# Statistics by VectorE for one batch, another order of first loads, centering in halves, and new written-out orders in a fused attention and FFN kernel

## The reference

```python
def layernorm(x):                       # over the last axis
    return (x - mean(x)) / sqrt(var(x) + 1e-5)

def mx_dequant(t):                      # blocks of 32 along the last axis
    scale = maximum(max_abs_of_block / 448, 1e-30)
    return (t / scale).astype(float8_e4m3fn).astype(float32) * scale

def attention(logits, ctx):
    q, k = ctx @ Wq.T + bq, ctx @ Wk.T + bk
    return logits @ softmax(q @ k.T).T  # x_m[l, m] = sum_n logits[l, n] * p[m, n]

def ffn(x, gate_w, up_w, down_w):
    linear = lambda a, w: mx_dequant(a) @ mx_dequant(w).T
    return linear(silu(linear(x, gate_w)) * linear(x, up_w), down_w)

x = x + attention(layernorm(x), ctx)
x = x + ffn(layernorm(x), gate_w, up_w, down_w)
```

## Time and profile before

| | us |
|---|---|
| median of 3 runs | 611.59 |
| lowest and highest | 611.04, 611.65 |
| profiled execution, its own time | 611.49 |
| span of its instructions | 609.7 |
| TensorE matmuls busy | 602.0 |
| VectorE busy | 485.4 |
| ScalarE busy | 308.9 |
| GpSimd busy | 48.8 |

### The profile page before, as it was taken

How to read it: one execution, slowest core, us unless ns; L and a number is a source line. 1 busy time by engine, 2 the same in 40 slices (tenths; PEclk the granted TensorE clock), 3 DMA queues, 4 the chain that set the end, 5 groups by cost and what they waited for, 6 DMA issues and landing times.

```text
span 609.7 us, 7213 instructions
## 1 busy us (share of the span) xinstructions
PE 602.0 (99%) x2690; PEld 282.8 (46%) x2690; DVE 485.4 (80%) x455; ACT 308.9 (51%) x463; POOL 48.8 (8%) x60
## 2 busy tenths in 40 slices
PE   8999999999999999999999999999999999999998
PEld 3455545444444444444444444444444444444446
DVE  5998998899999979899899997231148989799940
ACT  3989989553455545863572642421212512644521
POOL 0000100201100100102001100000000000110000
PEclk9999999999999999999999999999999999999999
DMA  8967989989888868775566668600110452856681
GB/s 326 384 144 263 293 229 213 258 216 250 207 206 207 209 135 176 172 158 130 130 118 140 162 140 147 137 4 15 18 19 0 90 86 51 137 90 102 119 141 34
DMA packets 148162, 92.28 MB, mean 151 GB/s; under 512 B 134304, under 2 KB 134688, under 8 KB 143264
## 3 DMA queue, kind: packets, MB, share of 16 engines
q1 hardware_dynamic: 142656, 63.78, 44.5%
q0 software_dynamic: 5472, 28.05, 19.8%
HBM read 25.76 MB, written 8.39 MB: 56 GB/s over the span
## 4 chain that ended last, share of the span: by engine, by line
PE 89%; ACT 7%; DMA 2%; issue 1%; SPq 0%; DVE 0%; DVEq 0%; ACTq 0%
PE bank L713 54%; PE bank L725 17%; PE bank L728 8%; PE bank L697 5%; PE bank L744 2%; ACT h L952 1%; DMA W<-hT 1%; PE bank L688 1%; ACT h L943 1%; PE bank L673 1%; DMA gu_lo<-in_consts 1%; PE bank L681 1%; ACT hT L932 1%; ACT mag L908 1%; ACT hT L994 0%
## 5 line engine op out<-in xcount | busy, mean ns | idle before, releaser
L713 PE MATMUL bank<-gu_hi,xT 128*128 128x512 f16 x1024 | 243.5, 379 | 1.0 <-DVE gu_hi L1440 1.0
L713 PEld LDWEIGHTS bank<-gu_hi,xT 128*128 128x128 f16 x1024 | 100.1, 98 | 122.2 <-issue 1.8
L713 PE MATMUL bank<-gu_lo,xT 128*128 128x512 f16 x512 | 131.4, 379 | 0.0
L725 PE MATMUL bank<-dn,hT 128*128 128x512 f16 x480 | 106.0, 379 | 0.0
L1569 DVE SCALAR_TENSOR_TENSOR h<-bank,unscale,silu 128x512 f32<-128x512 f32 x64 | 47.1, 747 | 58.8 <-PE bank L713 50.7
L1049 ACT ACTIVATE silu<-bank,unscale 128x512 f32<-128x512 f32 x64 | 42.9, 679 | 91.0 <-PE bank L713 38.3
L713 PEld LDWEIGHTS bank<-gu_lo,xT 128*128 128x128 f16 x512 | 50.1, 98 | 60.4
L725 PEld LDWEIGHTS bank<-dn,hT 128*128 128x128 f16 x480 | 47.0, 98 | 56.6
L1075 ACT ACTIVATE W<-h 128x2048 f16<-128x2048 f32 x16 | 30.6, 1911 | 65.7 <-issue 19.9
L697 PE MATMUL bank<-dn,h 128*128 128x512 f32 x128 | 56.0, 593 | 0.0
L728 PE MATMUL bank<-dn,hT 128*128 128x512 f16 x240 | 54.2, 379 | 0.0
(11 more groups left out here) (115 smaller groups left out, 552.8 us busy)
## 6 DMA issues: line engine op xcount, KB each, us to landing
W<-hT POOLq DMA_DIRECT2D x12, 1024.0 KB, 5.8
W<-in_units SPq DMA_DIRECT2D x11, 1024.0 KB, 6.0
h<-W POOLq DMA_DIRECT2D x7, 1024.0 KB, 5.8
h<-in_xcols SPq DMA_DIRECT2D x4, 1024.0 KB, 13.2
out_y<-y POOLq DMA_DIRECT2D x15, 256.0 KB, 4.9
h<-in_xrows SPq DMA_DIRECT2D x2, 1024.0 KB, 14.8
out_y<-h SPq DMA_DIRECT2D x2, 1024.0 KB, 7.7
h<-hT POOLq DMA_DIRECT2D x2, 1024.0 KB, 6.0
```

The costliest lines, as they stand in the source:

```text
L713: last = pe.matmul(bank[:, :], xT[:, b % 2, part, k, :], w[:, c, g, j * 512:(j + 1) * 512], start=(j == 0 and not low), stop=(j == HT - 1 ...
L725: pe.matmul(bank[:, :], hT[:, r % 2, 0, k, :], dn[:, w, k, :], start=(k == 0 and w == 0), stop=False)
```

## The change

It does the following.

- The row mean and variance of batch 3 come from VectorE's statistics instructions (`row_stats(3)`); ScalarE makes only the Ln and Exp of them (`row_root_of_stats(3)`).
- ctx 0 and the constants, now one DMA instead of two, are loaded ahead of unit 0. Fillers at the start: 8 for 18.
- `row_means`, `row_variances`, `center_by_scalar` and `attended_variances` of ScalarE are called in halves of two tiles, with a wait where two of them use the same scratch columns.
- `down_last` does the high-part matmuls of both halves first and waits for the low part after them.
- The lists of all engines and `bank_uses` are in a new order, with five fillers `keep("t2.1", 5)` before `turn_probs(2, 1)`.

```diff
+    stats_by_vector = (3,)
+        def means_made(b):
+            return 1 + sum(n not in stats_by_vector for n in range(b))
...
             def load_consts():
-                sp.dma_start(wts, consts[:, 0:514]).then_inc(consts_in, 16)
-                sp.dma_start(idf, consts[:, 514:514 + P]).then_inc(consts_in, 16)
+                sp.dma_start(late[:, 1024:1538 + P], consts).then_inc(consts_in, 16)
...
+            load_ctx(0)
+            load_consts()
             load_half(0)
             load_rest(0)
-            load_ctx(0)
-            load_consts()
             load_ctx(1)
             load_unit(1)
+            load_ctx(2)
+            load_ctx(3)
             load_rows(0)
-            load_ctx(2)
+            load_rows(1)
             load_unit(2)
-            load_ctx(3)
+            load_rows(2)
             load_columns(0)
-            load_rows(1)
-            load_rows(2)
             load_columns(1)
+            load_rows(3)
...
-            sp.wait_ge(*rows_rest_in(0))
+            sp.wait_ge(*unit_rest_in(2))
             turn_rows_hi(0)
             turn_rows_lo(0)
             turn_unit_hi(2)
...
+            turn_unit_lo(3)
             turn_unit_hi(3)
-            turn_unit_lo(3)
+            turn_rows_hi(1)
             load_unit(6)
             store_rows(3)
             sp.wait_ge(*unit_rest_in(4))
-            turn_rows_hi(1)
             turn_rows_lo(1)
...
             pool.wait_ge(wT_in[0], 32)
+            rows_rest(0)
             unit_rest(2)
             unit_max(3)
-            rows_rest(0)
...
             def down_last():
                 r = RT - 1
-                bank = take_bank(f"d{r}")
+                halves = [take_bank(f"d{r}")]
                 pe.wait_ge(hT_in[0], 16 * (r + 1))
-                pe.wait_ge(hT_in[1], 16 * (r + 1))
                 for part in range(2):
                     cols = slice(part * H // 2, (part + 1) * H // 2)
                     if part == 1:
                         pe.wait_ge(down_taken, r)
-                        bank = bank_of(f"d{r - 1}")
+                        halves.append(bank_of(f"d{r - 1}"))
                     for k in range(IT):
-                        for a, w in ((0, 0), (0, 1), (1, 0)):
-                            last = pe.matmul(bank[:, cols], hT[:, r % 2, a, k, :], dn[:, w, k, cols], ...
+                        for w in range(2):
+                            pe.matmul(halves[part][:, cols], hT[:, r % 2, 0, k, :], dn[:, w, k, cols], ...
+                pe.wait_ge(hT_in[1], 16 * (r + 1))
+                for part in range(2):
+                    cols = slice(part * H // 2, (part + 1) * H // 2)
+                    for k in range(IT):
+                        last = pe.matmul(halves[part][:, cols], hT[:, r % 2, 1, k, :], dn[:, 0, k, cols], ...
                     last.then_inc((half_ready, down_ready)[part], 1)
...
-            keep_zeros(18)
-            pe.wait_ge(consts_in, 32)
+            keep_zeros(8)
+            pe.wait_ge(consts_in, 16)
...
             product(3, 0)
             product(1, 0)
-            product(0, 0)
             attend(3, 0)
             attend(3, 1)
             attend(3, 2)
+            product(0, 0)
             attend(3, 3)
             product(2, 0)
...
+            def row_root(b, variances, scale):
+                act.wait_ge(act_step, own.done(
+                    nc.scalar.activation(xlog[:, of(b)], variances, ACT.Ln, scale=scale, bias=eps[:, 0:1])))
+                nc.scalar.activation(xrstd[:, of(b)], xlog[:, of(b)], ACT.Exp, scale=-0.5).then_inc(xrstd_ready, 1)
+            def row_root_of_stats(b):
+                act.wait_ge(xstats_ready[b], 1)
+                row_root(b, mv[:, of(b), 1], 1.0)
...
+            def row_stats(b):
+                dve.wait_ge(x_in[b], 16)
+                for lt in range(LT):
+                    last = dve.bn_stats(stats[:, LT * b + lt, :], X[b][:, lt * H:(lt + 1) * H])
+                then(last)
+                for lt in range(LT):
+                    last = dve.bn_aggr(mv[:, LT * b + lt, :], stats[:, LT * b + lt, :])
+                then(last)
+                dve.tensor_scalar(xnmean[:, of(b)], mv[:, of(b), 0], -1.0, None, ALU.mult).then_inc(xstats_ready[b], 1)
```

More of the change, by code:

```diff
@@ L998, in attended_variances @@
                                                     accum_out=ysum[:, row])
-                act.wait_ge(act_step, own.done(last))
+                own.done(last)
+                if half == 0:
+                    return
+                act.wait_ge(act_step, own.n)
                 if b in logged:
@@ L1018, in center_by_scalar @@
                 src = X[b] if b < 2 else late_xw
-                for lt in range(LT):
+                for lt in range(2 * half, 2 * half + 2):
                     cols = slice(lt * H, (lt + 1) * H)
@@ L1639, in _ @@
             row_max(2, 1)
[L1640 removed]
+            unit_round(1)
+            add_attended(0, 0)
+            row_sum(1)
+            unit_dequant(1)
             unit_scale(2)
[L1642 to L1644 removed]
             add_attended(0, 1)
[L1646 removed]
+            row_max(2, 2)
             add_attended(0, 2)
[L1648 to L1651 removed]
@@ L1652, in _ @@
-            attended_means(0)
-            center(0)
-            row_max(2, 3)
-            rows_scale(0)
-            unit_dequant(2)
-            add_attended(1, 0)
-            row_sum(2)
+            add_attended(0, 3)
+            row_max(2, 3)
+            attended_means(0)
+            row_max(3, 0)
+            unit_round(2)
+            center(0)
+            row_sum(2)
+            rows_scale(0)
+            unit_power(2)
             unit_reduce(3)
             rows_round(0)
+            row_max(3, 1)
@@ L1661, in _ @@
+            rows_dequant(0)
+            unit_largest(3)
+            add_attended(1, 0)
             add_attended(1, 1)
-            unit_largest(3)
-            rows_dequant(0)
-            add_attended(1, 2)
-            row_max(3, 0)
-            row_max(3, 1)
             row_max(3, 2)
             row_max(3, 3)
+            unit_dequant(2)
+            add_attended(1, 2)
             unit_scale(3)
-            row_sum(3)
             add_attended(1, 3)
             unit_reduce(4)
+            row_sum(3)
@@ L1682, in _ @@
-            rows_scale(1)
+            rows_round(1)
             unit_power(4)
-            add_attended(2, 3)
-            unit_reduce(5)
-            rows_round(1)
-            rows_dequant(1)
-            unit_round(4)
-            unit_dequant(4)
-            add_attended(3, 0)
-            add_attended(3, 1)
-            hidden_of(3, 0)
+            rows_dequant(1)
+            add_attended(3, 0)
+            hidden_of(3, 0)
+            unit_round(4)
+            add_attended(3, 1)
+            unit_dequant(4)
```

589 lines of the change are left out of this document (306 added, 283 removed).

## The result

The changed kernel takes 613.13 us (median of 20 executions, 612.27 to 616.72) against 611.87 for the kernel before (20 executions on the same chip, 610.62 to 612.98). The ratio is 1.0032, 95% interval 1.0020 to 1.0044. The forecast was 609.4, range 607.8 to 612.0: wrong in direction and outside its range. The profiled execution of after took 612.37 us with a span of 610.6; before's took 611.49 with 609.7. So the profiles account for 0.9 us of the 1.26 between the medians. The other 0.4 lie in how the executions spread: 13 of after's executions lie at 612.3 to 613.5, all but one of them with a mean granted clock of 1.000 (the other 0.999), and 7 at 614.1 to 616.7 with 0.994 to 0.997. Before has none above 613.

The account below looks back on a forecast made before the run. TensorE, busy 602.0 of 609.7 us, was taken as the bound. Gains of 1.2 (product(3,0) earlier) and 1.0 (wait before product(2,0)) took 611.49 to 609.3, with 0.1 for handovers 609.4; range 607.8 to 612.0.

Parts of the forecast that it names:

- Front: Start of the kernel: projections from 5.7, ctx 1 at 10.2 to 10.4, project(1,0) 2.1 us earlier, row_max(0,0) at 15.5.
- The clock: First projections: after eight fillers TensorE may still run at 1.2 GHz, leaving 0.7 us gained, time 610.8.
- ScalarE's chain: Attention stage: 1.9 us less work before take_probs(2,3), ending at 71.6 to 74.2, up to 76; product(3,0) at 89 to 93.
- TensorE's chain: Attention stage to product(3,0): 80.9 us of unchanged work plus 1.1 of filler from 10.2, so product(3,0) at 92.2.
- The filler: keep("t2.1", 5) before turn_probs(2,1): ten passes of 0.11, 1.1 us, counted whole though it might lie in a wait.
- The turned rows: Batch 0's rows before product(3,0): unit_dequant(2) ends at 76.1 to 78.5, so product(3,0) at 91.1 to 93.5, latest chain.
- rival C: Slower through batch 0's turned rows: unit_dequant(2) four late at 82.5, product(3,0) at 97.5, time 613.7; chance 0.11.
- Statistics: Batch 3's statistics: ScalarE loses 5.8 us, VectorE gains 3.3 (2.1 to 4.4), hidden with 4 us of cover.
- Attend(3) ahead: Attend(3) before product(0,0): the 1.02 us wait before product(2,0) goes, 1.0 gained; take_probs(3,3) at 101, needed by 103.4.
- After 125 and the tail: From 124.7 on: 0, up to 1.5 us of loss; the tail behind down_last: 0, bounds 0 to +0.4.
- Rival B: Gain swallowed by the low clock, new ScalarE gaps up to 76 or a wait after 124.7: 610.4 to 612; chance 0.22.

Follow-up runs that it names:

- u2: The changed kernel with plain copies in place of its transposing transfers, nothing else changed: 613.44 us, ratio 1.0031 to the kernel before.
- u1: The kernel before with plain copies in place of its transposing transfers, nothing else changed: 611.57 us, ratio 1.0001 to the kernel before.
- u4: The kernel before with plain copies, and ctx 0 and the constants loaded ahead of unit 0, still 18 fillers: 613.54 us, ratio 1.0033.
- v3: The changed kernel with plain copies, without keep("t2.1", 5), energies(3,2) and (3,3) put back as covers before attend(1,0) and attend(2,0): 613.43 us, ratio 1.0018.
- v2: The changed kernel with plain copies, and ctx 1 loaded ahead of unit 0: 613.94 us, ratio 1.0030.
- w2: The changed kernel with plain copies, no keep filler, energies as covers, old load order, 18 fillers, batch 3's means and variances back on ScalarE: 616.00 us.
- u3: The changed kernel with plain copies and 18 fillers at the start instead of 8: 612.96 us, ratio 1.0016.
- v1: The changed kernel with plain copies and without the filler keep("t2.1", 5): 612.27 us, ratio 1.0008.
- w1: The changed kernel with plain copies, no keep filler, energies as covers, old load order, 18 fillers, rows_hi(0) and row_means(2,1) moved behind take_probs(2,3): 613.80 us.
- x2: The kernel before with plain copies, add_attended(3,0) and (3,1) moved ahead of unit_dequant(4), and batch 3's statistics on VectorE: 610.81 us, ratio 0.9982.

## Why the prediction was wrong

- **Front, right in kind, mis-sized.** The first projection at 5.36 (forecast 5.7) held. ctx 1 was forecast at 10.2 from 325 to 384 KB/us; project(1,0) started at 11.22 in after, and in the stand-ins with its loads and eight fillers at 10.96 to 12.21. In the kernel before it started at 12.42 (the prediction's sum has 12.32). The gain on TensorE was 1.2, not 2.1, and in u2's profile, with the fallen clock, nothing was left of it: energies(0,0) came at 15.47, 14.03 in u1. The rate fell with the new order; before, then after, from 4 to 8 us (last column GB/s):
```profile
4.00:8.00 4.00, 3.39 (x12) 1.18 (x10) 2.87 (x5) 0.00 (x0) 0.00 (x0) 1.00 0.99 346
```
```profile
4.00:8.00 4.00, 3.42 (x5) 1.18 (x4) 0.00 (x0) 0.00 (x0) 0.00 (x0) 1.00 0.92 295
```
  With the load order alone changed the fall is larger; u1, then u4:
```profile
4.00:8.00 4.00, 2.81 (x12) 1.03 (x10) 2.90 (x5) 0.00 (x0) 0.00 (x0) 1.00 0.97 351
```
```profile
4.00:8.00 4.00, 4.00 (x13) 1.68 (x12) 0.00 (x0) 0.00 (x0) 0.00 (x0) 1.00 0.80 216
```
  The reductions of unit 0's halves started at 8.56 and 9.88 (landings forecast: 7.3 and 8.84), row_max(0,0) at 16.48 instead of 15.5. Why the rate falls was not tried.
- **The clock, half right.** The text foresaw the low level in the first passes and priced it at 1.4 us. In after's profile it stood there and cost nothing, since ctx 1 was late anyway. What can cost is the fall after a wait: 3.13 us in u2, 2.35 in v3, 2.13 in v2 and 2.58 in w2 were followed by 0.50; waits of 1.38 to 1.56 for ctx 1 in u3, u4 and v1 were not, nor those of 1.67 in v3 and of 1.96 and 1.97 behind the fillers in w1 and u1. The prediction had no such fall in its sum. That executions come in two sorts fits the rule of the Trainium skill cited there ("TensorE: Matmul & The Clock Gate", Part 1), by which the moment differs from run to run; but ctx 1, too, landed anywhere from 10.96 to 12.21 in the profiles, and no run tells the two reasons apart.
- **ScalarE's chain, the step that failed.** "It ends between 71.6 and 74.2, up to 76": take_probs(2,3) ended at 77.62. The step added and subtracted ScalarE's work ahead of it and took its idle time as something the new order would hardly enlarge. The idle time grew, from 2.5 to 4.7 us of the 60, and 3.5 us of it were take_probs waiting for TensorE; against that row (fourth pair: ScalarE):
```profile
16.00:76.00 60.00, 58.41 (x210) 31.82 (x209) 57.80 (x73) 55.30 (x127) 2.79 (x5) 1.00 0.81 254
```
  Up to the end of take_probs(2,3) ScalarE had 1.0 us less work from 16 us on (56.5, before 57.6) and ended 1.5 us later. From there the prediction's distance held: product(3,0) came 17.5 us after it, against the 18.2 less 0.9 of the sum.
  TensorE's chain, too, was counted "80.9 us of work, the same in the new order", with no wait, and the filler. From project(1,0) at 11.22, 1.0 later than forecast, to product(3,0) it had 80.3 us of work, 1.2 of filler and 2.43 of waits for take_probs, for which the sum had nothing. Two of the waits (0.84 each) are the handover through take_probs left bare by moving energies(3,x) ahead. At the other two places TensorE's part was long done and ScalarE was late: 0.75 before the filler (turn_probs(2,0) ended at 68.7, take_probs(2,0) at 72.8), and, behind product(3,0), 0.92 before attend(3,0). Putting the covers back (v3) gained nothing, so the missing covers were the place of the loss and not its cause: v3 and w1 show ScalarE, and behind it VectorE, unable to serve a faster TensorE. In short, the step that failed is to have added up each engine's chain by itself: in the new order TensorE and ScalarE waited for each other in turn, 2.4 and 3.5 us, where the forecast had no wait for the one and 2.5 us of idle time for the other.
- **The filler.** Counted whole, 1.1; v1 shows 0.72 (its forecast of 0.9 to 1.2 was too high as well). It stood behind the wait for the bank that take_probs(2,0) frees, so it did not lie in that wait.
- **The turned rows.** Forecast latest of the chains, with unit_dequant(2) done by 78.5: 78.64, the turns at 87.00 and 90.70, no wait. Right; rival C did not occur.
- **Statistics.** 2.46 + 0.38 + 0.17 = 3.0 us on VectorE, 3.3 forecast; hidden, as said.
- **Attend(3) ahead, the second step that failed.** The wait of 1.02 went, as said. But attend(3,0) needed take_probs(3,3) by 103.4, forecast 101, real 106.4. "5.8 us more of ScalarE work before it" was taken off in full, though 3.0 of them only became idle time, for ScalarE waits at take_probs(3,0) for attend(2). The 0.92 us before attend(3,0) ate the gain.
- **After 125 and the tail.** Forecast 0: +0.01, and 3.0 us of tail as before. x2's new wait shows how near product(6,0) was.

Against the sum: -1.2 was +0.90, -1.0 was -0.04, 0 was +0.01. Rival B, "swallowed", named the mechanisms (low clock, new gaps of ScalarE) and bounded them at 612, too low, because it kept the 1.0 us of product(2,0) whole. I had given 0.11 to slower, all of it to rival C.

## What to carry to other kernels

Before a piece of ready work is moved ahead, ask which handover between engines it covered, and whether the engine at the other end can go faster at all. Don't add up each engine's chain by itself: where several engines are within about 1 us of each other, a new order is no gain by itself. Work taken off an engine counts only up to the next point where that engine waits for something else: look for the buffer or bank it will stand at. When one wait has one cause (here a 0.7 us addition behind a 2.3 us dequantization), try the small move first, and look at what the work moved back was feeding. A stand-in that replaces a transfer by a quicker one can't judge a change whose margin is that transfer.

## What the runs showed of the hardware

- Four statistics of 128x512 take 2.46 us (0.61 each) on VectorE, four aggregations 0.38, so 0.7 a piece, as much as a reduction (0.68). ScalarE's root waited 0.52 us for the last of them, ahead of 3.00 us in which it stood anyway.
- After waits of 2.13 to 3.13 us (v2, v3, w2, u2) TensorE's granted clock was 0.50 in the next stretches (1.2 GHz), and in u2 the four passes of project(1,0) took 3.43 us instead of 1.88. In w2 the fall cost no time, since ScalarE was later still. The Trainium skill, "TensorE: Matmul & The Clock Gate", Part 1, has the low level as the default that activity lifts; these rows agree, and show besides that a stretch at full speed ahead of the wait did not keep the high level.
- The same transfers in another order moved 216 instead of 351 GB/s from 4 to 8 us (u4, u1).
- Plain copies of 512 KB in place of the transposing transfers took 3.8 instead of 5.0 us from issue to landing at batch 0's turns (medians of two, u1 and the kernel before).
